# Negated row maxima of two attention layers: from diagonal products and selections to a row inside stacks loaded by DMA

## What is computed

```python
# third layer: causal softmax attention
logits = jnp.einsum('bhsd,bhtd->bhst', q, k) * scale
logits = jnp.where(mask, logits, neg_inf)
probs = jax.nn.softmax(logits, axis=-1)
out = jnp.einsum('bhst,bhtd->bhsd', probs, v)
# fourth layer: the same, and one rotary product shared by all heads
scores = jnp.einsum('bqhd,bkhd->bhqk', q, k)
scores = scores + jnp.einsum('bqr,bkr->bqk', q_rope, k_rope)[:, None]
scores = scores / scale
w = jax.nn.softmax(jnp.where(causal, -jnp.inf, scores), axis=-1)
```

## Time and profile before

| | us |
|---|---|
| median of the runs shown (lowest, highest) | 2587.52 (2585.28, 2588.34) |
| the profiled execution | 2591.79 |
| its span, first to last instruction | 2590.0 |
| third layer's attention stage | 1173 to 1608 |
| fourth layer's attention stage | 1809 to 2379 |
| busy over the whole span: TensorE, ScalarE, VectorE, GpSimd | 2029.6, 1590.5, 1579.7, 1141.4 |

### The profile page before, as it was taken

The page is one execution under the profiler, slowest core; times in us unless marked ns, Lnnn a source line. Parts: engine busy times, 40 slices in busy tenths (PEclk is TensorE's granted clock), DMA queues, the critical chain, the costliest instruction groups (busy, mean ns, idle before and its releaser), DMA issues.

```text
span 2590.0 us, 66263 instructions
## 1 busy us (share of the span) xinstructions
PE 2029.6 (78%) x23246; PEld 1391.6 (54%) x23247; DVE 1579.7 (61%) x3648; ACT 1590.5 (61%) x3690; POOL 1141.4 (44%) x930
## 2 busy tenths in 40 slices
PE   1553899999999788437889886853899999997993
PEld 0223566666666566334555554633566666665662
DVE  2236788787887888764554454766444544443775
ACT  0231577676777455206988897530788888886552
POOL 0002577664555233314854554330466654333552
PEclk9785899999999899856787786985999999998997
DMA  8900000020000111200020000220000000000224
GB/s 224 170 0 0 12 17 17 18 77 3 2 2 2 41 46 47 82 24 14 22 67 2 2 2 6 53 62 8 11 17 18 16 12 2 2 2 10 64 62 124
DMA packets 109678, 88.19 MB, mean 34 GB/s; under 512 B 11240, under 2 KB 95816, under 8 KB 109424
## 3 DMA queue, kind: packets, MB, share of 16 engines
q1 hardware_dynamic: 97840, 60.82, 10.3%
q0 software_dynamic: 11584, 23.91, 2.7%
HBM read 45.26 MB, written 39.43 MB: 33 GB/s over the span
## 4 chain that ended last, share of the span: by engine, by line
PE 44%; DVE 21%; ACT 14%; issue 12%; POOL 6%; DMA 2%; DVEq 1%; SPq 1%; ACTq 0%; POOLq 0%
PE duo L1023 9%; PE mo L1023 9%; PE misc L1023 8%; PE ob L1023 6%; PE acc L1023 6%; PE pt L1023 4%; ACT qT L865 3%; POOL v L643 3%; ACT v L903 3%; ACT v L902 2%; DVE nmax L2084 2%; DVE v L1805 2%; DVE region L2087 1%; DVE nmax L1974 1%; ACT L902 1%
## 5 line engine op out<-in xcount | busy, mean ns | idle before, releaser
L643 POOL TENSOR_TENSOR v<-v 128x768 f16<-128x768 f32 x256 | 419.6, 1639 | 545.5 <-ACT v L903 544.4
L638 POOL TENSOR_TENSOR v<-v 128x512 f16<-128x512 f32 x256 | 290.3, 1152 | 259.2 <-DVE region L2087 259.0
L865 ACT ACTIVATE qT<-small_ident,nmax 128x128 f16<-128x128 f32 x1024 | 328.9, 404 | 58.7 <-DVE nmax L1974 57.5
L665 POOL DMA_INDIRECT results<-probT,dest_no x202 | 217.2, 1075 | 330.2 <-ACT probT L704 290.9
L1973 DVE TENSOR_REDUCE nmax<-duo 128x2 f32<-128x256 f32 x256 | 108.4, 423 | 391.5 <-PE duo L1023 391.1
L1023 PE MATMUL ob<-wm,v 128*128 128x9 f16 (+1 forms) x5856 | 255.8, 180 | 82.7 <-POOL v L643 62.9
L1023 PEld LDWEIGHTS ob<-wm,v 128*128 128x128 f16 x5856 | 222.7, 98 | 144.4 <-POOL v L643 84.3
L964 ACT ACTIVATE v<-mo 128x512 f32<-128x512 f32 x256 | 153.4, 599 | 159.3 <-PE mo L1023 159.3
L1023 PE MATMUL duo<-kT,wm 128*128 128x256 f16 x1212 | 173.3, 280 | 54.8 <-DVE kT L1793 28.8
L2084 DVE TENSOR_REDUCE nmax<-duo 128x2 f32<-128x512 f32 x256 | 164.8, 685 | 83.4 <-PE duo L1023 83.4
L1023 PE MATMUL mo<-qT,kT 64*128 64x256 f16 (+1 forms) x2240 | 200.6, 271 | 0.0
(11 more groups left out here) (279 smaller groups left out, 4726.6 us busy)
## 6 DMA issues: line engine op xcount, KB each, us to landing
prob<-slot_rows SPq DMA_DIRECT2D x101, 130.0 KB
qT<-results SPq DMA_DIRECT2D x40, 256.0 KB, 3.1
slot_rows<-prob SPq DMA_DIRECT2D x4, 1300.0 KB, 20.6
slot_rows<-prob SPq DMA_DIRECT2D x4, 1235.0 KB, 22.2
xd<-in_L_ffn_w_dram SPq DMA_DIRECT2D x2, 2048.0 KB, 12.1
results<-probT,dest_no POOLq DMA_INDIRECT x202
slot_rows<-xd,slot_no POOLq DMA_INDIRECT x160, 2.4
x<-in_L_attn_x_dram SPq DMA_DIRECT2D x8, 256.0 KB, 4.6
```

The source lines that it names most:

```text
L638: pool.tensor_tensor(p16[:, p % 2, h, 1, :], p32[:, h, :], p16[:, p % 2, h, 0, :], ALU.subtract)\
L643: pool.tensor_tensor(p16_2[:, p % 2, 1, :], p32_2[:, p % 2, :], p16_2[:, p % 2, 0, :], ALU.subtract)\
L665: pool.indirect_dma_start(out=results[layer], out_offset=bass.IndirectOffsetOnAxis(ap=dest_no[:, 2 * b + t:2 * b + t + 1], axis=0), in_=y_ ...
L865: ins = act.activation(diag2[:, p % 2, n // 2, n % 2, :], small_ident[:, :], ACT.Copy, scale=nmax4[:, p % 2, n:n + 1])
```

## The change

The diagonals, the selections and ScalarE's part in them go. A head's stack gets a block of rows for the maximum: in the keys a row of ones, in the queries a row that is zero while the maxima are made and holds the negated maxima when the scores are. One product a head and tile then gives scores with the maximum subtracted.

- `turn_maxima` (TensorE): at even steps, for two steps' maxima (16-bit, `nm16`), two products with the identity turn four columns each into rows. `turn_rows` (VectorE) copies the 4x256 row into `nm_rows` (in `xnT`). `send_rows` (SP) puts it into the stacks by one DMA. In the third layer the turned row stands in the bank `misc`, in the fourth in free columns of `duo`.
- The maxima run 6 steps ahead in the third layer and 4 in the fourth (`LEAD`), in place of 2. TensorE's order is scores(p), turn, average(p-1), maxima(p+LEAD).
- The parts of q and k are written to a DRAM tensor `head_rows` (three DMAs each), and the stacks are loaded from there by group and side (`feed_attention`, eight loads a chunk). In the third layer a stack stays four heads of 32 rows. In the fourth each head has its own 128 rows: 96 rotary rows, the same for all heads, broadcast from SBUF by a second DMA, and 32 of its own; the rotary product falls away.
- `prepare` moves to steps 2, 3, 5 (third layer) and 3 to 8 (fourth), the third layer's output product to step 7, the shared expert to steps 9 to 12 and 10 to 13.
- The fourth layer's expert weights (2 x 2 MB) are loaded from ScalarE's queue before the last chunk of the third layer's attention, in place of SP's after its 32nd step. The selection matrices that GpSimd built are gone.

```diff
-        SELECT_AT = {0: (2, 3), 2: (4,), 4: (5,), 6: (6,), 8: (7,)}
-        SHARED_AT = {1: 0, 3: 1, 5: 2, 7: 3}
-        DOWN_AT = {4: 0, 5: 1, 7: 2, 8: 3}
-        PREPARE = range(9, 14)
+        SHARED_AT = {9: 0, 10: 1, 11: 2, 12: 3}
+        DOWN_AT = {10: 0, 11: 1, 12: 2, 13: 3}
+        PREPARE = range(2, 10)
+        LEAD = {2: 6, 3: 4}
+        REFILL = {2: 2, 3: 4}
...
+        def ahead(layer, p, more):
+
+            n = p + LEAD[layer]
+            return (0, n) if n < STEPS else (1, n - STEPS) if more else None
+
+        def rows_ahead(layer, p, more):
+
+            e = (p + LEAD[layer] - 2) // 2
+            if p % 2 or e < 0:
+                return None
+            return (0, e) if e < 8 else (1, e - 8) if more else None
...
+                def put_rows(n, kind):
+
+                    if n:
+                        for g in range(4):
+                            sp.wait_ge(stack_in[g], stack_count(layer, n))
+                    proj_read_v.wait(sp, stage, n, low_made[kind])
+                    for b, plane in enumerate(planes[kind]):
+                        sp.dma_start(head_rows[kind][:, b + 1, :, :], parts[:, plane, :]).then_inc(rows_put[kind], 16)
+
+                def load_heads(n, g, kind):
+
+                    if n:
+                        s_full.wait(sp, stage, n - 1, 8 * g + 7)
+                    if layer == 3:
+                        proj_read_v.wait(sp, stage, n, rope_made[kind])
+                        sp.dma_start((head_q, head_k)[kind][g][0:HEAD0, :, :],
+                                     rope[kind][0:HEAD0, :].rearrange("p (o c) -> p o c", o=1)
+                                     .broadcast_to([HEAD0, 4, CHUNK])).then_inc(stack_in[g], 16)
+                    sp.wait_ge(rows_put[kind], put_count(layer, n + 1))
+                    own = head_rows[kind][4 * g:4 * g + 4]
...
+                def send_rows(i, e):
+
+                    g, b = e // 2, e % 2
+                    nm_turned.wait(sp, stage, i, e)
+                    own = slice(SEQ * b, SEQ * (b + 1))
+                    dst = q_stack[0:P:GROUP, g, own] if layer == 2 else head_q[g][HEAD0:HEAD0 + 1, :, own]
+                    sp.dma_start(dst, nm_rows[:, b, :]).then_inc(nm_in[b], 16)
...
+                put_at = {2: {2: 0, 4: 1}, 3: {4: 0, 6: 1}}[layer]
+                next_at = {2: {6: both[0:2], 8: both[2:4], 12: both[4:6]},
+                           3: {7: both[0:1], 9: both[1:2], 11: both[2:3], 13: both[3:4], 14: both[4:5], 15: both[5:6]}}[layer]
+                last_at = {2: {0: both[6:8]}, 3: {0: both[6:7], 2: both[7:8]}}[layer]
...
+                for i in range(NCH):
+                    more = i < NCH - 1
+                    for p in range(STEPS):
+                        at = rows_ahead(layer, p, more)
+                        if at:
+                            send_rows(i + at[0], at[1])
+                        for g, kind in (last_at if i else first_at).get(p, ()):
+                            load_heads(i, g, kind)
+                        if more:
+                            if p in put_at:
+                                put_rows(i + 1, put_at[p])
+                            if p in next_at:
+                                s_full.wait(sp, stage, i, 2 * p)
+                            for g, kind in next_at.get(p, ()):
+                                load_heads(i + 1, g, kind)
...
-                def diagonals(i, p):
-
-                    nmax_made.wait(act, stage, i, p)
-                    for n in range(4):
-                        ins = act.activation(diag2[:, p % 2, n // 2, n % 2, :], small_ident[:, :], ACT.Copy,
-                                             scale=nmax4[:, p % 2, n:n + 1])
-                    ins.then_inc(diag_made.sem, 1)
...
-                def maxima(i, parity, p):
+                def rows_of(g, jj, h):
+
+                    if layer == 2:
+                        r = head(g, jj, h)
+                        return q_stack[r, g, :], k_stack[r, g, :]
+                    return head_q[g][:, 2 * jj + h, :], head_k[g][:, 2 * jj + h, :]
+
+                nm_bank = [misc[0:4, 0:P], misc[0:4, P:SEQ]] if layer == 2 else                     [duo[0:4, 0, LINE:CHUNK], duo[0:4, 1, LINE:CHUNK]]
+
+                def turn_maxima(i, e):
+
+                    nmax_made.wait(pe, stage, i, 2 * e + 1)
+                    if layer == 2:
+                        at_step(nm_turned, pe, stage, i, e - 1)
+                    for qt in range(2):
+                        ins = mm(nm_bank[qt], nm16[:, e % 2, 4 * qt:4 * qt + 4], ident_h[:, :], True, True)
+                    ins.then_inc(nm_full.sem, 1)
+
+                def maxima(i, p):
 
                     g, b, jj = pair2(p)
                     if p % 4 == 0:
-                        stacked.wait(pe, stage, i, 2 * g + 1)
+                        pe.wait_ge(stack_in[g], stack_count(layer, i + 1))
                     at_step(nmax_made, pe, stage, i, p - 1)
+                    if layer == 3 and p % 2 == 0:
+                        at_step(nm_turned, pe, stage, i, p // 2 - 1)
                     q0, k0 = SEQ * b, SEQ * b
-                    if layer == 3:
-                        q, k = after["q"][parity], after["k"][parity]
-                        for h in range(2):
-                            mm(duo[:, h, 0:P], q[:, q0:q0 + P], k[:, k0:k0 + P], True, False)
-                            mm(duo[:, h, P:LINE], q[:, q0 + P:q0 + SEQ], k[:, k0:k0 + SEQ], False, False)
                     for qt in range(2):
                         for h in range(2):
-                            r = head(g, jj, h)
-                            mm(duo[:, h, P * qt:P + SEQ * qt], q_stack[r, g, q0 + P * qt:q0 + P * qt + P],
-                               k_stack[r, g, k0:k0 + P + P * qt], layer == 2 and qt == 0, False)
+                            q, k = rows_of(g, jj, h)
+                            mm(duo[:, h, P * qt:P + SEQ * qt], q[:, q0 + P * qt:q0 + P * qt + P], k[:, k0:k0 + P + P * qt],
+                               qt == 0, False)
                     for h in range(2):
-                        mm(own_tiles(duo[:, h, 0:LINE]), ident16[:, :], twice(mask16[:, :]), False, True)                            .then_inc(max_full.sem, 1)
-
-                def scores(i, parity, p):
+                        mm(own_tiles(duo[:, h, 0:LINE]), ident16[:, :], twice(mask16[:, :]), False, True)\
+                            .then_inc(max_full.sem, 1)
+
+                def scores(i, p):
 
                     g, b, jj = pair2(p)
-                    diag_made.wait(pe, stage, i, p)
+                    if p % 2 == 0:
+                        pe.wait_ge(nm_in[b], rows_count(layer, i, p // 2))
                     q0, k0 = SEQ * b, SEQ * b
-                    for h in range(2):
-                        u = 2 * p + h
-                        dst = trio[u % 3]
-                        at_step(p_high, pe, stage, i, u - 3 if u >= 3 else u - 2)
-                        mm(dst[:, 0:SEQ].rearrange("p (a c) -> p a c", a=2), sixteen16[:, :], diag2[:, p % 2, :, h, :],
-                           True, False)
-                        mm(dst[:, SEQ:LINE], sixteen16[:, :], diag2[:, p % 2, 1, h, :], False, False)
-                        mm(own_tiles(dst[:, 0:LINE]), mask16[:, :], twice(ident16[:, :]), False, False)
-                        if layer == 3:
-                            q, k = after["q"][parity], after["k"][parity]
-                            mm(dst[:, 0:SEQ], k[:, k0:k0 + P], q[:, q0:q0 + SEQ], False, False)
-                            mm(dst[:, SEQ:LINE], k[:, k0 + P:k0 + SEQ], q[:, q0 + P:q0 + SEQ], False, False)
                     for kt in range(2):
                         for h in range(2):
-                            r = head(g, jj, h)
-                            ins = mm(trio[(2 * p + h) % 3][:, SEQ * kt:SEQ + P * kt],
-                                     k_stack[r, g, k0 + P * kt:k0 + P * kt + P], q_stack[r, g, q0 + P * kt:q0 + SEQ],
-                                     False, kt == 1)
-                            if kt:
-                                ins.then_inc(s_full.sem, 1)
+                            u = 2 * p + h
+                            if kt == 0:
+                                at_step(p_high, pe, stage, i, u - 3 if u >= 3 else u - 2)
+                            q, k = rows_of(g, jj, h)
+                            mm(trio[u % 3][:, SEQ * kt:SEQ + P * kt], k[:, k0 + P * kt:k0 + P * kt + P],
+                               q[:, q0 + P * kt:q0 + SEQ], kt == 0, False)
+                    for h in range(2):
+                        mm(own_tiles(trio[(2 * p + h) % 3][:, 0:LINE]), mask16[:, :], twice(ident16[:, :]), False, True)\
+                            .then_inc(s_full.sem, 1)
...
+                def turn_rows(i, e):
+
+                    nm_full.wait(dve, stage, i, e)
+                    sent = rows_count(layer, i, e - 2)
+                    if not (isinstance(sent, int) and sent == 0):
```

(22 more changed lines are left out.)

324 lines of the change are left out of this document (193 added, 131 removed).

## The result

| kernel | median us | lowest to highest | ratio to before, 95% interval |
|---|---|---|---|
| before | 2587.9 | 2585.3 to 2592.4 | |
| changed | 2568.0 | 2563.0 to 2572.1 | 0.9927 (0.9911 to 0.9943) |

The sign was right, the size was not: 20 us came out of a forecast 65, and 2568 us lies inside the stated range of 2450 to 2592, 24 us from its slow end. The change in time is 0.7%, with an interval of 0.6 to 0.9%.

A forecast was written before the change was run, and what follows sets the result against it. With ScalarE and TensorE relieved, a circle through four engines was taken to bound the steps. Third layer -6 and fourth -59 us gave -65, so 2526.8 for the profiled execution and 2522 us for the median; range 2450 to 2592.

The forecast's parts named there:

- The third layer's clock share: Third-layer attention: 30% of the time at full clock, a guess, mixing 44.3 and 52.8 us into 50 us a chunk.
- The circle: Exponentials, GpSimd's low half, average, maxima, scores bound two steps: third layer 5.1 us at full clock, 6.0 at half; fourth 5.2.
- the work beside the circle: Third layer, a chunk: projections, transposes and evacuations added to the steps, 4.3 + 0.5 us at half clock.
- The fourth layer's plain steps: Fourth-layer attention: twelve steps a chunk other than the Gelu steps take 2.6 us each, 31.2 together.
- The rotary chain: Fourth layer: VectorE's 3.3 us rotary arithmetic delays the row's copy, so 9.7 us of TensorE work a chunk counts whole.
- The order of maxima and average: TensorE, both layers: maxima, now behind the average, counted in the sum for two steps, 0.55 us in the fourth layer.
- Rival 2: Clock falls in both layers: third at half +17 us, fourth 63.5 us a chunk, sum -18, 2569 us; chance 0.14.
- Rival 1: Clock holds at 2.4 GHz in the third layer: third -51 us, fourth -59, 2477 us; chance 0.20.
- Rival 3: Fourth layer's row DMA lands late, 4.6 us against 2.6 that fit: +96 us, 2618 us; chance 0.14.
- The diagonals: ScalarE, 20.8 us a chunk removed: worth next to nothing in plain steps (2.67 against 2.6), full length in four Gelu steps.
- The starts: Stage starts: third layer +12 us, 1 of it back at the end; fourth layer +3 us.
- Two signs: Signs in the profile after: third-layer clock between 0.6 and 0.7; fourth-layer average waiting for GpSimd in most steps.

The follow-up runs named there:

- e3: Changed kernel plus, in the third layer, two useless TensorE products a step ahead of each average, maxima still behind it: 2567.3 us, ratio to before 0.9933.
- e9: Changed kernel plus, in the third layer, four useless TensorE products a step ahead of the average, maxima still behind it: 2527.4 us, ratio to before 0.9767.
- e7: Changed kernel with VectorE's fourth-layer rotary chain cut in two, copy and subtraction moved behind the next step's copy of the row and its maxima: 2529.0 us, ratio 0.9782.
- e1: Changed kernel with the third layer's attention put back to the code of before, so only the fourth layer is changed: 2544.9 us, ratio to before 0.9834.
- e8: Changed kernel with the fourth layer's 96 shared stack rows loaded in the first chunk only, not in the seven others: 2567.7 us, ratio to before 0.9936.
- e11: Changed kernel with third-layer maxima first and four fillers, fourth-layer rotary chain cut, and three fillers in fourth-layer steps 10 to 15 and 0 to 2: 2453.6 us, ratio 0.9500.
- e5: Changed kernel with, in the third layer, maxima ahead of the average and four useless products a step between them: 2502.0 us, ratio to before 0.9669.
- e13: Changed kernel plus three useless products ahead of the average in fourth-layer steps 10 to 15 and 0 to 2, rotary chain uncut: 2570.4 us, ratio 0.9946.
- e12: Changed kernel with GpSimd making the low part of one head's probabilities only, in both layers, part of the computation left out: 2484.4 us, ratio to before 0.9612.
- e2: Changed kernel with the third layer's maxima issued ahead of the average instead of behind it: 2544.1 us, ratio to before 0.9831.
- e10: Changed kernel with third-layer maxima first and four fillers a step, and the fourth layer's rotary chain cut in two: 2460.2 us, ratio to before 0.9517.
- e14: Changed kernel with third-layer maxima first and three fillers a step, fourth-layer rotary chain cut, and fourth-layer fillers in steps 10 to 15 and 0 to 2: 2457.4 us, ratio 0.9513.

## Why the forecast was wrong, step by step

**The third layer's clock share, the step that failed.** Between the prices of 44.3 us a chunk at full clock and 52.8 at half stood "I take 30% at full, a guess". The granted clock of 0.57 means 14%, and the measured chunk, 53.1, lies at the half-clock end: 3.1 us above the 50 forecast, 25 us in all. The share is half of that: with 14% the forecast's own formula gives 51.4. The other 1.7 us are the prices. If 44.3 is kept for full clock, 53.1 at a share of 14% asks for 54.9 at half (an estimate from these figures), 2.1 above the 52.8. The circle in it was right (5.95 us for two steps), which leaves the work beside the circle as the part priced too low; no run takes it by itself. The argument behind the guess pointed the right way (TensorE has 30% less to do, and the clock had fallen before without a long wait) and was followed only halfway. e3 and e9 show the cause of the low clock: with as many columns as were removed put back, the clock returns most of the way to where it was; with twice as many, it stays at 2.4 GHz.

**The fourth layer's plain steps, the term that was too small.** The rotary chain was priced well: 9.7 us of projection work counted whole in place of half is 4.9 us a chunk for the chain, and e7, which cuts it, gives 39 / 8 = 4.9. The size was partly luck, for the chain's own waits are 2.6 us of it (1.28 in each of steps 6 and 8), and the clock behind the wait and the long subtraction, which the forecast did not have, are the rest.

What is missing lies elsewhere. With the chain 60.5 was forecast and 62.6 to 64.1 measured, and without it 55.7 ("if only half of the 9.7 shows") and 58.1: some 2 to 3 us are missing in both. From exponentials to exponentials, in the mean of seven chunks of the changed kernel, steps 3 to 8 take 25.5 us (26.4 to 26.6 in e1, e8 and e9) where 15.6 + 9.7 = 25.3 were counted. The six steps 13 to 15 and 0 to 2 take 17.7 us where 15.7 were (six times 2.6, less 1, with 0.8 and 0.3), and e7 leaves them at 17.7: a plain step is 2.95 us in the mean, not 2.6. The clock is up to 0.5 us of these two (17.2 in e11); step 1 also holds the output product of the chunk before, which the forecast had in its 9.7. The Gelu steps add 0.3 to 0.4.

**The order of maxima and average, not weighed at all.** The forecast noted "maxima, now behind the average" and used it in the sum, but never asked what the old order would give. It is worth 24 us as the kernel stands and, with the clock kept up, 25 (e9 to e5).

**Rival 2** named 2569 us, and 2568 was measured. It is right in the third layer (+17 forecast, +13 by the profiles, +23 by e1). In the fourth it gave 63.5 a chunk, 3 of it by a fallen clock; the size is right and the cause is so for about 1 us only (e13 and e11), so its 2569 is in part luck. **Rival 1** (clock at 2.4 GHz in the third layer) is what e9 makes by hand. **Rival 3** did not happen: no wait for a row's transfer stands in either stage, and e8 takes the reloads out without effect that can be told.

**What held.** The circle in the third layer: 5.95 us for two steps against 6.0, and e12 shortens both layers, with the reserve made there. The diagonals are worth nothing in a plain step (2.95 us in the mean now, 2.67 in the earlier trace rows) and nearly their full length in a Gelu step: two of them in the changed kernel, start to start 4.96 us (4.85 forecast, 6.10 in the earlier trace rows):

```profile
2150.47 0.49 ACT L1019 ACTIVATE v<-mo 128x384 f32<-128x384 f32 x1
...
2155.43 0.49 ACT L1019 ACTIVATE v<-mo 128x384 f32<-128x384 f32 x1
```

The starts: +10.6 us in the third layer (+12 forecast, though its own terms, 1.5 + 4.6 + 8.0 - 3.5, add up to 10.6); in the fourth the first exponentials come at 1850.06 against 1832.88 before, 17.2 later, of which the third layer's end accounts for 13.8 (1618.50 against 1604.71): +3.4, where +3 was forecast. ScalarE at 51% (below 70% forecast). Two signs did not hold: the clock stands below the 0.6 to 0.7 of the forecast, and the average waits for GpSimd in about half of the steps, not in most (56 waits in the 114 steps of 1220 to 1600 us, 64 in the 114 of 1885 to 2330).

**What stays open.** The runs do not say what it is in the filler that the clock answers to, the number of products, their 128 rows or the shorter waits: fillers of 32 rows, the height of this stage's own products, were not tried on the chip. Open are also the fourth layer's plain steps, 2.95 us against 2.6, of which the clock explains a small part, and in the third layer the 1.7 us a chunk that the share does not explain.

## What to carry to other kernels

Where TensorE's granted clock is below 1 in the rows of before, work taken off TensorE can cost time: price the stage at both clocks, and take the lower one unless a row shows the clock holding at the lower load. Then try useless products in the waits; here they are worth 41 us alone, and 66 with the order repaired, of which some 25 are the order's. When a load is removed from one engine, write down the circle that is left, and ask of each link whether it must stand in it: the maxima need not have. A copy that another engine waits for goes ahead of a long chain on its engine, and the wait is followed further before it is priced: to the engine after the next, to the clock that TensorE has behind it, and to what another engine does during the chain. A chunk is read from all its repetitions, since here step 8 took 5 us in some and 9 in others.

## What the runs showed of the hardware

The granted clock of TensorE can stay at or near 1.2 GHz for some 400 us while the profile shows the engine busy for over 90% of the time: in e2 379 of 390 us at 0.51 (1200 to 1590 us), in the changed kernel 373 of 410 at 0.56 (1200 to 1610). The longest wait of a product for another engine is 1.4 us in the first and 1.5 in the second. The busy share of the profile does not tell that the clock will hold. The Trainium skill, TensorE: Matmul & The Clock Gate, section "A second HAM failure mode: psum-queue depth-cycling", says that short idles between groups of products make the clock swing between its two levels. The changed kernel's third layer agrees, but the swings are short: most windows of 10 us from 1170 to 1630 us stand at 0.50, as the one shown, and the highest at 0.84, which makes 0.57 over 280 us. It swings more with two fillers (e3: windows of 20 us between 0.50 and 1.00), and it stands at 1.00 with four.

The other way round, work added to the engine on the critical circle shortened it: in the same window of 280 us, e9 issues 3519 matrix instructions and the changed kernel 2740, of which some 390 are fillers in e9 (four a step, 16 steps a chunk), and e9 gets through six chunks where the changed kernel gets through 5.3.

An instruction of VectorE and one of GpSimd can lengthen each other. The subtraction of 32x512 on VectorE, 0.68 us otherwise, took 2.60 or 2.00 beside GpSimd's subtraction of 128x768 in three of seven chunks of the changed kernel, and GpSimd's took up to 2.19 in place of 1.64 in the other four. In e7, e10, e11 and e14, with the chain cut, VectorE's was never long.
